# A two-layer graph kernel on one core: TensorE's product order changed to G, V, scores, Z, P·V, Z·W, with the first layer's result moved into its own step

## The reference, cut to what matters

```
h  = relu(layernorm(x))
q, k, v = h @ Wq.T + bq, h @ Wk.T + bk, h @ Wv.T + bv
p  = adj * exp(q @ k.T)
x1 = x + (p / p.sum(-1)) @ v
h1 = relu(layernorm(x1))
A  = adj + I;  d = A.sum(-1) ** -0.5;  L = A * d[:, None] * d[None, :]
out = x1 + L @ (h1 @ W + b)
```

## Time and profile before

| | us |
|---|---|
| median of the runs | 1633.65 |
| the profiled execution | 1633.5 |
| its span | 1631.7 |
| TensorE busy | 1622.8 |
| VectorE busy | 1346.4 |
| ScalarE busy | 1075.2 |
| GpSimd busy | 802.1 |

### The profile page before, as it was taken

One profiled execution on the slowest core, in us unless ns is written; L12 is line 12 of the kernel. 1 busy time (PEld: TensorE's weight loads), 2 busy tenths in 40 slices (PEclk: granted clock), 3 DMA queues, 4 the chain that ended last, 5 costly groups with the idle time before them and its releaser, 6 DMA issues.

```text
span 1631.7 us, 37843 instructions
## 1 busy us (share of the span) xinstructions
PE 1622.8 (99%) x12061; PEld 1544.9 (95%) x12061; DVE 1346.4 (83%) x3370; ACT 1075.2 (66%) x2450; POOL 802.1 (49%) x970
## 2 busy tenths in 40 slices
PE   9999999999999999999999999999999999999999
PEld 7899999999999999999999999999999999999998
DVE  6888888888888888888888888888888888888886
ACT  5676666666766766766766667667667667666663
POOL 3545544544554455455445445544554554454452
PEclk9999999999999999999999999999999999999999
DMA  5455455455455464464554554554644545545531
GB/s 184 115 128 153 124 124 151 116 134 150 109 144 133 109 159 126 117 156 122 124 151 117 133 150 109 143 133 109 158 125 118 154 124 124 151 118 133 146 89 49
DMA packets 494559, 212.66 MB, mean 130 GB/s; under 512 B 402512, under 2 KB 427344, under 8 KB 494544
## 3 DMA queue, kind: packets, MB, share of 16 engines
q1 hardware_dynamic: 492624, 210.89, 50.2%
q10 hardware_dynamic: 1920, 1.58, 0.3%
HBM read 146.28 MB, written 66.13 MB: 130 GB/s over the span
## 4 chain that ended last, share of the span: by engine, by line
PE 95%; DVE 3%; SPq 1%; issue 1%; ACT 0%; DMA 0%; POOL 0%; POOLq 0%; DVEq 0%; ACTq 0%
PE ps L982 32%; PE ps L984 31%; PE ps L985 31%; SPq L180 1%; DMA adj_blocks<-in_adj_dram 0%; DVE ht_lo L779 0%; DVE wt_lo L664 0%; DVE unused_a L941 0%; DVE g_lo L675 0%; DVE m_lo L626 0%; DVE w_lo L669 0%; DVE z_lo L762 0%; DVE wt L651 0%; SPq L210 0%; DVE late L795 0%
## 5 line engine op out<-in xcount | busy, mean ns | idle before, releaser
L454 ACT ACTIVATE g_hi<-ps,u_col 128x256 fp32r<-128x256 f32 x256 | 106.0, 465 | 310.0 <-PE ps L985 310.0
L309 POOL TENSOR_TENSOR xb<-xb,bv_row 128x512 f32<-128x512 f32 x128 | 163.5, 1299 | 275.1 <-DVE late L768 271.9
L982 PE MATMUL ps<-ht_hi,m_hi 128*128 128x256 f32 x1024 | 287.0, 280 | 2.0 <-DVE ht_lo L779 1.8
L984 PE MATMUL ps<-ht_lo,m_hi 128*128 128x256 f32 x1024 | 286.6, 280 | 0.0
L985 PE MATMUL ps<-ht_hi,m_lo 128*128 128x256 f32 x1024 | 286.3, 280 | 0.0
L982 PE MATMUL ps<-w_hi,z_hi 128*128 128x512 f32 (+1 forms) x516 | 203.1, 394 | 0.7 <-DVE z_lo L762 0.7
L985 PE MATMUL ps<-w_hi,z_lo 128*128 128x512 f32 (+1 forms) x516 | 202.8, 393 | 0.0
L984 PE MATMUL ps<-w_lo,z_hi 128*128 128x512 f32 (+1 forms) x516 | 202.5, 392 | 0.0
L982 PEld LDWEIGHTS ps<-ht_hi,m_hi 128*128 128x128 f32 x1024 | 193.2, 189 | 2.4 <-issue 2.0
L985 PEld LDWEIGHTS ps<-ht_hi,m_lo 128*128 128x128 f32 x1024 | 193.2, 189 | 0.0
L984 PEld LDWEIGHTS ps<-ht_lo,m_hi 128*128 128x128 f32 x1024 | 193.2, 189 | 0.0
(11 more groups left out here) (165 smaller groups left out, 5507.0 us busy)
## 6 DMA issues: line engine op xcount, KB each, us to landing
x_in<-in_x_dram SPq DMA_DIRECT2D x64, 512.0 KB, 5.1
xb<-in_x_dram SPq DMA_DIRECT2D x64, 512.0 KB, 4.5
out_dram<-late SPq DMA_DIRECT2D x127, 256.0 KB, 2.1
h_scratch<-h SPq DMA_DIRECT2D x62, 512.0 KB, 2.8
h_blocks<-h_scratch SPq DMA_DIRECT2D x248, 128.0 KB, 3.9
adj_in<-in_adj_dram SPq DMA_DIRECT2D x64, 256.0 KB, 3.0
adj_blocks<-in_adj_dram SPq DMA_DIRECT2D x256, 64.0 KB, 2.5
dn_row<-dn_scratch SPq DMA_DIRECT2D x64, 128.0 KB, 2.9
```

What stands on the lines that cost most here:

```text
L309: last = pool.tensor_tensor(xb[:, t, :], xb[:, t, :], bv_row[:], ALU.add)
L454: last = act.activation(g_hi[:, m, :], ps[:, G + j, m % 2 * N:m % 2 * N + N], ACT.Identity, bias=u_col[:, m:m + 1])
L982: pe.matmul(dst, a_hi[:, c, cols], b_hi[:, c, :], start=(first and c == 0), stop=False, skip_group_check=not first)
L984: pe.matmul(dst, a_hi[:, c, cols], b_lo[:, c, :], start=False, stop=False, skip_group_check=not first)
```

## The change

It does the following.

- From step 3 on TensorE's order is G, V, S, Z, PV, W instead of G, V, Z, S, W, PV. PV of these steps is put in banks 6, 7, 0, 1. In loop steps G waits also for `x1_ready[1]` of the graph before.
- On DVE, z_lo moves behind p_lo; `keep_x1` and bn_stats of graph k move into step k, behind z_lo; then come `x_variance` of graph k+2, the sums of L, ht_lo of graph k+1, `x_shift` of graph k+2 and the two results. The next step begins with d, bn_aggr and ve_1.
- On ACT, z_hi and `x_squares` move behind p_hi.
- Step 3 is written out (`third`): keep_adjacency, g_hi, the adjacency transpose, turn_dn, the sums of L and the adjacency DMA have other places in it.
- In step 2, V6 waits for the first half of `ht_sum_lo` only, v_p1 and v_p5 are copied earlier, ht_lo is made before x1, and POOL's block sums wait for ht_lo.
- The drain loses 14 matmuls whose result is unused, and its sums of L and biases move behind z_lo.

The diff, cut to its core (bodies that only move into the functions `sums_of_l`, `neighbours` and `scores`, and signatures, are left out):

```diff
 HT = (2, 4)
-O = (6, 2)
+O_EARLY, O = (6, 2), (6, 0)
 VA, VB, VC, VD = 4, 5, 6, 7
...
     step(2, prev=True, main=True, ahead=True, older=False)
-    with eng.Fori(3, B - 1) as this:
+    step(3, prev=True, main=True, ahead=True, third=True)
+    with eng.Fori(4, B - 1) as this:
         step(this, prev=True, main=True, ahead=True)
...
+    def load_adj(this):
+        adj_next = adj_flat[bass.ds(sp.snap(this * (N * N)), N * N)]
+        sp.wait_ge(rsum_ready, this)
+        sp.dma_start(adj_in[:], adj_next.rearrange("(t p n) -> p t n", p=P, n=N)).then_inc(adj_loaded, 16)
+
...
                 sp.dma_start(out[this - 3, t * P:(t + 1) * P, :], y[:, t, :]).then_inc(stored, 16)
-        if main and ahead:
-            adj_next = adj_flat[bass.ds(sp.snap(this * (N * N)), N * N)]
-            sp.wait_ge(rsum_ready, this)
-            sp.dma_start(adj_in[:], adj_next.rearrange("(t p n) -> p t n", p=P, n=N)).then_inc(adj_loaded, 16)
+        if main and ahead and not third:
+            load_adj(this)
         if prev and ahead:
...
             load_x(this)
+        if third:
+            load_adj(this)
         if main:
...
             sp.wait_ge(adjt_ready, this)
         if second and not prev:
...
+    def x1_power(graph):
+        pool.wait_ge(ve_1_done, graph)
+        pool.tensor_tensor(rs_1[:], ve_1[:], minus_half[:], ALU.pow).then_inc(rs_1_done, 1)
+
...
             if main:
-                ht_sums_low(this)
+                ht_sums_low_half(this, 0)
+                if third:
+                    x1_power(this - 1)
+                    pool.wait_ge(ln_1_ready, this - 1)
+                ht_sums_low_half(this, 1)
             hat_low(this - 1, older)
...
             ht_sums_low_half(this, 0)
-        if prev and main:
-            pool.wait_ge(ve_1_done, this - 1)
-            pool.tensor_tensor(rs_1[:], ve_1[:], minus_half[:], ALU.pow).then_inc(rs_1_done, 1)
+        if prev and main and not third:
+            x1_power(this - 1)
         if prev and not older:
+            pool.wait_ge(ln_1_ready, this - 1)
             ht_sums_low_half(this, 1)
...
             pool.wait_ge(dn_turned_ready, this - 1)
+            if third:
+                pool.wait_ge(sd_ready, this - 1)
             row_norms(this)
...
             pool.wait_ge(v_done[V3], this)
+            if prev and not older:
+                pool.wait_ge(ht_lo_ready[1], this + 1)
             ht_sums(this + 1)
...
                 ht_sums_high(this)
-            keep_adjacency(this, True)
+            if not third:
+                keep_adjacency(this, True)
         if prev and older:
...
             act.wait_ge(u_ready, 1)
-        if main and (not prev or older):
+        if main and (not prev or older) and not third:
             g_high(0, this)
...
+            if main and not older:
+                keep_p1(this)
             for t in range(NT):
...
                 if main and not older and t == 0:
-                    keep_p1(this)
+                    keep_p5(this)
+                if third:
+                    (keep_p1 if t == 0 else keep_p5)(this)
+            if third:
+                keep_adjacency(this, True)
+                g_high(0, this)
         if main:
-            if not prev or older:
+            if (not prev or older) and not third:
                 keep_p1(this)
...
             if prev and not older:
-                keep_p5(this)
                 g_high(0, this)
             g_high(1, this)
-            if not prev or older:
+            if (not prev or older) and not third:
                 keep_p5(this)
...
                 layer_norm_x(this, prev, older)
-            elif second:
+            elif second and older:
                 x_sums(this + 2)
...
                 z_high(this - 1)
+                x_sums(this + 2)
+                x_squares(this + 2)
             act.wait_ge(v12_ready, this)
...
             wt_high()
-        if prev and older:
+        if prev and not main:
             z_high(this - 1)
...
             act.activation(v_hi[:, 1, :, 0:HD], v[:, 1, :, 0:HD], ACT.Copy).then_inc(v_hi_ready[2], 1)
-            if second and prev:
-                x_squares(this + 2)
             for t in range(NT):
...
                 act.activation(p_hi[:, t, :], p[:, t, :], ACT.Copy).then_inc(p_hi_ready[t], 1)
+        if main and prev and older:
+            z_high(this - 1)
+            if second:
+                x_squares(this + 2)
         if main and ahead:
...
-    def keep_x1(t, graph):
+    def sums_of_l(graph, prev):
...
+    def keep_x1(t, graph, banks=O):
+        bank = banks[t]
         dve.wait_ge(o_done[t], graph)
...
             h1_low(0, this - 1)
+            dve.wait_ge(stored, (this - 3) * (16 * NT))
+            result(0, this - 2, d)
+            h1_low(1, this - 1)
             result(1, this - 2, d)
-            h1_low(1, this - 1)
             dve.wait_ge(y_ready[0], this - 2)
             dve.wait_ge(y_ready[1], this - 2)
-            dve.wait_ge(sd_ready, this - 1)
-            add_bias(0, this - 1)
-            add_bias(1, this - 1)
         if prev and main:
-            dve.wait_ge(xb_ready, this - 1)
-            for t in range(NT):
-                keep_x1(t, this - 1)
-                last = x1_stats(t, this - 1)
-                if not older:
+            if not older:
+                dve.wait_ge(xb_ready, this - 1)
+                for t in range(NT):
+                    keep_x1(t, this - 1, O_EARLY)
+                    last = x1_stats(t, this - 1)
                     (x_variance if t == 0 else x_shift)(this + 1)
-            last.then_inc(bn_1_done, 1)
+                last.then_inc(bn_1_done, 1)
             if older:
...
             dve.tensor_scalar(ve_1[:], mv_1[:, :, 1], EPS, None, ALU.add).then_inc(ve_1_done, 1)
-            transpose_adjacency(this, prev)
+            if not third:
+                transpose_adjacency(this, prev)
             dve.wait_ge(d_ready, this - 1)
...
                                      ALU.mult).then_inc(ln_1_ready, 1)
-            if older:
+            if third:
+                sums_of_l(this - 1, True)
+            elif older:
                 turn_dn(this, prev)
                 g_low(0, this)
-            h1_low(0, this - 1)
-            add_bias(0, this - 1)
             if not older:
                 value_u2(this)
+                w_low(slice(0, 2))
+            h1_low(0, this - 1)
+            if third:
+                dve.wait_ge(sd_ready, this - 1)
+            add_bias(0, this - 1)
             h1_low(1, this - 1)
+            if third:
+                transpose_adjacency(this, prev)
+                g_low(0, this)
             if not older:
...
             value_low(this)
-            w_low(slice(0, 2))
             z_low(this - 1)
...
             transpose_h(this)
+        if third:
+            turn_dn(this, prev)
         if ahead and not main:
...
                 x_mean(this + 2)
-        if prev and older:
+        if prev and not main:
             z_low(this - 1)
+        if prev and not main:
+            sums_of_l(this - 1, True)
+            dve.wait_ge(sd_ready, this - 1)
+            add_bias(0, this - 1)
+            add_bias(1, this - 1)
         if main:
...
             value_low_lower(this)
-            if second and prev:
+            if second and prev and not older:
                 x_variance(this + 2)
...
                 dve.tensor_tensor(p[:, t, :], e[:, t, :], adjt[:, t, :], ALU.mult).then_inc(p_ready[t], 1)
-            if second and prev and older:
-                x_shift(this + 2)
             p_low(this)
...
                 transpose_h(this)
-                x_shift(this + 2)
+                ht_low(this + 1, None)
+        if main and prev and older:
+            z_low(this - 1)
+        if main and prev and older and ahead:
+            dve.wait_ge(xb_ready, this)
+            dve.wait_ge(x1b_ready[1], this - 1)
+            dve.wait_ge(mv_1_done, this - 1)
+            for t in range(NT):
+                keep_x1(t, this)
+                last = x1_stats(t, this)
+            last.then_inc(bn_1_done, 1)
+            if second:
+                x_variance(this + 2)
         if main and not prev:
             ht_low(this + 1, HT[1])
-        if main:
...
+        if main and ahead and (not prev or older):
+            sums_of_l(this, prev)
+        if main and ahead and prev and older:
+            ht_low(this + 1, None)
+            if second:
+                x_shift(this + 2)
+        if main and prev and not older:
+            x_shift(this + 2)
+            dve.wait_ge(xb_ready, this)
             for t in range(NT):
-        if main and ahead and prev:
-            ht_low(this + 1, None)
+                keep_x1(t, this, O_EARLY)
+                last = x1_stats(t, this)
+            last.then_inc(bn_1_done, 1)
         if ahead and not main:
...
             x_mean(this + 2)
-        if prev and main:
+        if prev and main and ahead:
             if older:
...
```

(33 more changed lines are left out.)

49 lines of the change are left out of this document (25 added, 24 removed).

## The result

The changed kernel takes 1843.02 us in the median (1835.19 to 1854.0, four runs) against 1633.66 before (1633.39 to 1634.24): ratio 1.1286 [1.1271, 1.1301], 12.9% slower. Forecast were 1766 us and a range of 1690 to 1810. The direction is right, the time lies outside the range: of 209.4 us lost the forecast has 132.

A forecast was written before the change was run, and what follows sets the result against it. TensorE, busy 99% of the span and without waits in the loop, was taken as the bound. Sum: 1633.5 - 0.1 (front end) - 1.8 (drain) + 134 (loop) + 1.1 (part steps) = 1766.7, stated as 1766 us; range 1690 to 1810.

The forecast's parts named there:

- The ring: Loop steps, adjT to adjT: closed chain of 26.3 us against TensorE's 24.83; without meetings a rival at 1719 us, chance 0.20.
- DVE beside POOL: Loop steps: two POOL block sums meet v_lo and p, lengthening the chain by 0.8 us, bounds 0 to 1.04.
- the DMAs moved: Loop steps: the store of h and its block loads come later; cost taken as 0, bounds 0 and 1 us per step.
- The clock: Rival, loop steps: two waits per step bring half clock, 59 x 1.4 = 83 us, about 1849; chance 0.08.
- The ends: Front end and drain outside the loop steps: -0.1 us and -1.8 us.
- the front end: Steps 2 and 3: 4.5 us removed, 4.4 given back, about even at -0.1 us.
- `v_u2` waits 3.5 (forecast 3.4): Step 3: v_u2 stands behind g_lo on DVE, giving 3.4 us of wait, bounds 0 and 5.
- The drain: After the loop: 14 unused matmuls go and W of graph 63 covers x1, saving 1.8 us, at worst 0.

The follow-up runs named there:

- experiment 2: Changed kernel with POOL's four block sums ht_sum waiting for p_lo in the loop steps: 1718.70 us, ratio 1.0520.
- experiment 1: Changed kernel with x_variance between the two x1 halves and x_shift directly behind them on DVE: 1735.53 us, ratio 1.0623.
- experiment 3: Changed kernel with the edits of experiment 1 and experiment 2 together: 1641.46 us, ratio 1.0042.
- experiment 9: Changed kernel with the edits of experiment 8 and experiment 2 together: 1638.39 us, ratio 1.0028.
- experiment 4: Changed kernel with SP issuing the xb load ahead of the four block loads of h in the loop steps: 1782.18 us, ratio 1.0909.
- experiment 5: Changed kernel with 12 unused matmuls on TensorE before the wait for p_lo in the loop steps: 1822.11 us, ratio 1.1152.
- experiment 8: Changed kernel with DVE's x1 and its statistics moved behind the sums of L, x_variance, ht_lo and x_shift: 1725.17 us, ratio 1.0557.
- experiment 6: Changed kernel with the edits of experiment 3 and experiment 4 together: 1637.18 us, ratio 1.0019.
- experiment 7: Kernel of experiment 6 with step 3's g_hi ahead of h1 on ACT, g_lo and v_u2 ahead of the sums of L on DVE: 1636.41 us.

## Why the prediction was wrong in size

**The ring** was right. The step that carries the forecast, 26.3 us without meetings, measured 26.13 in experiment 2, and its places are those named: the layer norm of x waits for `nb_x`, adjT for `hat_lo`, V2 for `v_p1`. Shortening it by some 1.5 us brings 107.5 us by itself (experiment 1), and experiments 3 and 9, which get it below TensorE's step in different ways and keep the sums apart, bring the loss back all but whole. The mean steps of four runs split the loss of the loop, and set beside it what the forecast had:

| | mean step, us | more than the line above, x 59 | forecast |
|---|---|---|---|
| before | 24.83 | | |
| the ring, sums apart (experiment 2) | 26.26 | 84 | 87 |
| with meetings, xb in time (experiment 4) | 27.34 | 64 | 47 |
| with xb late, no half clock (experiment 5) | 27.99 | 39 | 0 |
| the change | 28.37 | 23 | 0 |

Experiment 2 still has a few steps with a late load, so that its mean is 0.13 above its median and the meetings look that much smaller in the third row.

**"DVE beside POOL"** failed: 0.8 us, bounds 0 to 1.04, "two block sums meet v_lo and p". Measured were 1.2 with xb in time (27.33 - 26.13, experiments 4 and 2), 1.5 in the undisturbed step shown, and up to 2.7 with a late xb (experiment 8). The size of one meeting, 0.52, was right (0.45, 0.55, 0.53); their number was right only with xb in time. I let POOL's block sums start where they did before. But x with bias starts when xb has landed, 6.6 us after adjT in the median instead of 6.06 before, and the first meeting also slows POOL: so three DVE operations meet sums, then four or five. The upper bound was no bound, since it counted places of the old timeline, and even the two meetings with xb in time pass it a little (1.2 against 1.04). The Trainium skill ("SBUF — State Buffer", section "SBUF: two separate sides") has VectorE with two SBUF inputs and GpSimd take turns for a whole instruction. The trace agrees: the long operations are those with two SBUF inputs, they lose 0.45 to 0.55 us per meeting, while v_lo of the first block, which reads PSUM, keeps its 0.41 beside a block sum (DVE at 1082.78). The rows also say why a meeting costs less than the whole block sum of 0.73, where the prediction took 0.52 for about one: what is lost goes with the part of the sum still to run. v lost 0.45 where 0.60 was left (1081.98), the second v_lo 0.55 and p 0.53 where 0.67 was left, and v of experiment 4 0.06 where 0.21 was left (1019.24). But by that rule too the sum is right only if the meetings are counted right.

**"Taken as 0, bounds 0 and 1 per step"**, the DMAs moved, failed. I checked h's block loads against the transposes; they were in time, 1.2 us ahead in the median. The load behind them on the same queue, xb, I did not follow to its user. Experiment 4 prices it: 61 us, 1.0 per step, of which 0.4 is the clock: the upper bound, where I had taken 0. This is the largest part of what the forecast missed.

**The second ring**, from PV over W and the second result to adjT and p_lo, is missing from the forecast. It bounds nothing in the change, where adjT waits for hat_lo in every step, and shows by itself only in experiment 8.

**The clock** was written as a rival of its own, with 0.08: a fall in each of 59 steps. It came as an addition: 17 falls, 21 to 23 us. The price of one, 1.4, was near (1.2 to 1.3). What failed is the form: ring, meetings, late load and clock are not cases that exclude each other but terms that feed each other, and a range made of exclusive cases ends too soon. With 3.0 us per step instead of 2.3 (an undisturbed step of 27.8) the same working gives 1633.5 - 0.1 - 1.8 + 177 + 1.1 = 1810, the end of the range; the falls and the spread are beyond it.

**The ends** were right in sum, the front end in part by luck. It is even as forecast (102.61 against 102.65). `ht_lo`'s wait of 1.8 and its half clock went, and G of step 3 starts 3.7 us earlier (72.52 against 76.20). Step 3 gives it back: `v_u2` waits 3.5 (forecast 3.4), and a half clock falls there too (84.9), which the forecast did not have. The drain gave 2.2 (1.8).

## What to carry to other kernels

When a link of a software pipeline moves, write down the closed chain from one operation to the same one a step later, over all engines, and compare its length with the bound engine's step; where it is longer, one short operation moved shortens it (experiment 1, 107 us), until the bound engine's own work is the longer of the two. Then redo the timeline of every engine whose work meets the moved work from its own new start, which may be a load's landing: a meeting's price can be read from the old trace, the number of meetings can't. Delays in one ring add up in one wait, and so do not show one by one in the list of waits; removing them one by one and together (experiments 1 to 5) shows what each was worth.

## What the runs showed of the hardware

**Half clock at short waits.** The clock fell in the loop at waits at PV of 1.7 to 2.9 us, in 17 steps, between 0.3 us ahead of PV's start and 1.6 us behind it. Other waits of up to 2.3 us in the same run brought none, nor did one of 2.7 in experiment 1 and one of 2.75 in experiment 8, where a wait of 2.5 did (1650.7); the waits of at most 1.3 us in experiment 4 brought none at all. So the length of the wait alone does not decide it, and what does is open. It costs time although TensorE is not the bound: 1.2 to 1.3 us of step each. With unused matmuls in the wait there was none (experiment 5).

**A step of 24.90 with nearly no wait.** In experiment 3 TensorE's step is 24.90 us, in experiments 6 and 9 24.94 in the mean, where it was 24.83 before. It is more than enough to keep experiment 6 above the kernel before (6.5 us in the loop). In that run G's 48 matmuls take 5.65 instead of 5.60 us and PV's 24 take 2.92 instead of 2.87 in the mean; why is open, and it wasn't tried.

**A wait is not its price.** In step 2 a wait of 1.8 us and a half clock went, step 3 started 3.7 us earlier, and a new wait of 3.5 with a half clock took 3.6 of it back. In experiment 7 that wait shrank by 3.1, and 0.8 at most came of it, since 2.4 stood at PV instead. Both times the waits are for DVE, and removing one moved it down DVE's queue.
